# Casting the next token tile one step early in both layernorms of an adaLN transformer block

## The reference

```python
x = L0_attn_x                                            # (4, 2048, 2048) f32
mod = (_silu(L0_c) @ L0_wmod).reshape(4, 6, 1, -1)       # wmod is (2048, 12288)
sa, ca, ga, sb, cb, gb = (mod[:, i] for i in range(6))
ga = (2 * (ga >= 0) - 1) * jnp.maximum(jnp.abs(ga), 0.25)   # gb likewise
h = _layernorm(x, axis=-1) * (1 + ca) + sa
x = x + ga * _L0_attn_ref(h, W_Q, W_K, W_V, W_O)
h = _layernorm(x, axis=-1) * (1 + cb) + sb
x = x + gb * _L0_ffn_ref(h, ...)                          # 8 experts, top 2, plus shared
```

## Time and profile before

| | us |
|---|---|
| runs of before | 4077.52 and 4167.37, median 4122.44 |
| the profiled execution | 4081.17 |
| its span on the slowest core, core 7 | 4079.6 |
| spans of all cores | 4064.4 to 4079.6 |
| TensorE busy | 3369.6 (83% of the span) |
| VectorE, ScalarE, GpSimd busy | 1119.1, 641.3, 468.9 |

### The profile page before, as it was taken

One profiled execution on the slowest core, in us unless ns is written; L12 is line 12 of the kernel. 1 busy time (PEld: TensorE's weight loads), 2 busy tenths in 40 slices (PEclk: granted clock), 3 DMA queues, 4 the chain that ended last, 5 costly groups with the idle time before them and its releaser, 6 DMA issues. The chain is left out here.

```text
span 4079.6 us, 46287 instructions; the slowest of 8 cores (4064.4 to 4079.6 us)
## 1 busy us (share of the span) xinstructions
PE 3369.6 (83%) x14394; PEld 1369.0 (34%) x14394; DVE 1119.1 (27%) x2039; ACT 641.3 (16%) x1312; POOL 468.9 (11%) x891
## 2 busy tenths in 40 slices
PE   3544688888888888888894399999999999999997
PEld 0232222222222222222242144444444444444443
DVE  0255322222222222222225412122121221212212
ACT  0233222222222222222203200000000000000000
POOL 1111000000000000000010012122121221212211
PEclk8666777777777777777796599999999999999998
DMA  9999310101010101010130054555455454544544
GB/s 210 155 174 170 67 16 16 16 16 16 16 16 16 16 16 16 16 16 16 16 63 16 3 80 73 75 76 77 73 74 75 74 76 73 73 78 72 76 73 119
DMA packets 128926, 246.51 MB, mean 60 GB/s; under 512 B 15681, under 2 KB 56770, under 8 KB 126402
## 3 DMA queue, kind: packets, MB, share of 16 engines
q0 software_dynamic: 125824, 209.92, 34.1%
q1 hardware_dynamic: 2882, 33.63, 2.4%
HBM read 444.94 MB, written 8.39 MB: 111 GB/s over the span
## 5 line engine op out<-in xcount | busy, mean ns | idle before, releaser
L570 PE MATMUL pacc<-h_full,rA 128*128 128x512 bf16 x2560 | 599.7, 395 | 18.0 <-DMA rA<-wk 18.0
L1268 PE MATMUL pdn<-ysb,rD 128*128 128x512 bf16 x2560 | 571.0, 387 | 13.1 <-DVE ysb L1212 11.3
L1158 PE MATMUL px<-h,rA 128*128 128x512 bf16 x2560 | 568.3, 380 | 0.8 <-ACT comb L347 0.8
L1183 PE MATMUL px<-h,rA 128*128 128x512 bf16 x2560 | 565.6, 379 | 0.0
L570 PEld LDWEIGHTS pacc<-h_full,rA 128*128 128x128 bf16 x2560 | 256.2, 101 | 347.0 <-issue 73.6
L1268 PEld LDWEIGHTS pdn<-ysb,rD 128*128 128x128 bf16 x2560 | 253.9, 99 | 328.7 <-issue 38.9
L1200 DVE TENSOR_TENSOR ysb<-x1s,px 128x1024 bf16<-128x1024 bf16 x80 | 97.7, 1221 | 961.0 <-PE px L1183 961.0
L1158 PEld LDWEIGHTS px<-h,rA 128*128 128x128 bf16 x2560 | 251.0, 98 | 305.2 <-issue 4.9
L1183 PEld LDWEIGHTS px<-h,rA 128*128 128x128 bf16 x2560 | 250.5, 98 | 302.1
L1278 DVE SCALAR_TENSOR_TENSOR x_own<-pdn,gbcl,x_own 128x512 f32<-128x512 f32 x320 | 240.1, 750 | 345.1 <-PE pdn L1268 345.1
L1172 ACT ACTIVATE x1s<-px 128x1024 bf16<-128x1024 f32 x80 | 81.9, 1024 | 1482.1 <-PE px L1158 1482.0
(11 more groups left out here) (153 smaller groups left out, 2363.6 us busy)
## 6 DMA issues: line engine op xcount, KB each, us to landing
rB<-wmodA POOLq DMA_DIRECT2D x96, 512.0 KB, 10.2
rA<-wg POOLq DMA_DIRECT2D x128, 256.0 KB, 4.8
rA<-wu POOLq DMA_DIRECT2D x128, 256.0 KB, 4.8
rD<-wd POOLq DMA_DIRECT2D x256, 128.0 KB, 5.2
xl<-ximg SPq DMA_DIRECT2D x16, 1024.0 KB, 5.3
rA<-wk POOLq DMA_DIRECT2D x32, 256.0 KB, 4.7
rA<-wq POOLq DMA_DIRECT2D x32, 256.0 KB, 4.7
rA<-wv POOLq DMA_DIRECT2D x32, 256.0 KB, 4.7
```

Of the source, the lines that this page charges most:

```text
L570: t.matmul(pacc[:, bank * 512:bank * 512 + 512], ub[:, (dc % 8) * 128:(dc % 8) * 128 + 128], moving_fn(dc, qtr), start=(dc == 0), stop=(dc ...
L1158: lambda t, ub=ub, dc=dc, half=half: t.matmul(px1[:, half * 512:half * 512 + 512], ub[:, (dc % 8) * 128:(dc % 8) * 128 + 128], h2[:, dc * ...
L1183: lambda t, ub=ub, dc=dc, half=half: t.matmul(px3[:, half * 512:half * 512 + 512], ub[:, (dc % 8) * 128:(dc % 8) * 128 + 128], h2[:, dc * ...
L1268: t.matmul(pdn[rot][:, :], ub[:, dloc * 128:dloc * 128 + 128], ysb[:, hc * 1024 + th * 512: hc * 1024 + th * 512 + 512], start=(hc == 0), ...
```

## The change

The cast and the square are taken out of `emit_ln_piece` and become a function of their own, `emit_ln_cast`. It is called once ahead of the loop, for tile 0, and then inside piece s for tile s+1, through `precast_fn`, between the copy into `rowbf` and the broadcast. Stage a of the mod half (`fill_fn`) moves from behind the square of the mean to the place behind the new cast. The load of tile s+1 is emitted ahead of piece s, with the same wait as before: on the end of VectorE's work of piece s-1. The second layernorm gets the same early cast, without a load. The cast waits for its load and for the matmuls that read `xbf` last.

```diff
+    def emit_ln_cast(x_src_ap, xbfb, xsqb, state, extra_waits=()):
+        w_cast = list(extra_waits)
         if state.get("stats_prev"):
             w_cast.append(state["stats_prev"])
-        s_c1 = em.op("scalar", lambda s: s.activation(xbfb[:, :], x_src_ap, AF.Copy),
-                     waits=w_cast, inc=True)
+        em.op("scalar", lambda s: s.activation(xbfb[:, :], x_src_ap, AF.Copy),
+              waits=w_cast, inc=True)
         s_c2 = em.op("scalar", lambda s: s.activation(xsqb[:, :], x_src_ap, AF.Square),
                      inc=True)
-        w_mm = [s_c2, misc["CG"]]
+        state["cast_mark"] = s_c2
...
         state["rows_read"] = s_m2
-        if fill_fn is not None:
-            fill_fn()
...
         s_cv = em.op("scalar", lambda s: s.copy(rowbf[:, :], rowa[0:1, 0:512]),
                      waits=w_bc, inc=True)
+        if precast_fn is not None:
+            precast_fn()
+        if fill_fn is not None:
+            fill_fn()
         g_bc = emit_bcast(rowbf[:, :], rows_b[:, :], pbc, waits=[s_cv], bf=True)
...
+    if SUB1 >= 2:
+        xw0 = ld_x(0)
+        emit_ln_cast(xl[0][:, :], xbf[:, :], xsq[:, :], ln1_state,
+                     extra_waits=[xw0])
+    for s_idx in (range(TC) if SUB1 >= 2 else range(0)):
+        slot = s_idx % 2
+        pc = None
+        if s_idx + 1 < TC:
+            xw = ld_x(s_idx + 1)
+            nslot = (s_idx + 1) % 2
+            pc = (lambda xw=xw, nslot=nslot:
+                  emit_ln_cast(xl[nslot][:, :], xbf[:, :], xsq[:, :],
+                               ln1_state, extra_waits=[xw]))
...
+    emit_ln_cast(x_own[:, 0:2048], xbf2[:, :], xsq2[:, :], ln2_state)
     for lc in range(LC):
         src = x_own[:, lc * 2048:(lc + 1) * 2048]
+        pc2 = None
+        if lc + 1 < LC:
+            pc2 = (lambda lc=lc: emit_ln_cast(
+                x_own[:, (lc + 1) * 2048:(lc + 2) * 2048],
+                xbf2[:, :], xsq2[:, :], ln2_state))
```

More of the change, by code:

```diff
@@ L348, in emit_bcast, with emit_ln_piece @@
         return s_b
-    def emit_ln_piece(x_src_ap, dst_fn, cvec, svec_col, prow_s, prow_q, state, rows_b, pbc, t1b, xbfb, xsqb, fill_fn=None, fill_fn2=None):
-        LD = state.get("x_ready")
-        w_cast = [LD] if LD else []
+    def emit_ln_cast(x_src_ap, xbfb, xsqb, state, extra_waits=()):
+        w_cast = list(extra_waits)
         if state.get("stats_prev"):
             w_cast.append(state["stats_prev"])
-        if state.get("cast_extra"):
-            w_cast.append(state["cast_extra"])
-        s_c1 = em.op("scalar", lambda s: s.activation(xbfb[:, :], x_src_ap, AF.Copy),
-                     waits=w_cast, inc=True)
+        em.op("scalar", lambda s: s.activation(xbfb[:, :], x_src_ap, AF.Copy),
+              waits=w_cast, inc=True)
         s_c2 = em.op("scalar", lambda s: s.activation(xsqb[:, :], x_src_ap, AF.Square),
                      inc=True)
-        w_mm = [s_c2, misc["CG"]]
+        state["cast_mark"] = s_c2
+    def emit_ln_piece(x_src_ap, dst_fn, cvec, svec_col, prow_s, prow_q, state, rows_b, pbc, t1b, xbfb, xsqb, fill_fn=None, fill_fn2=None, precast_fn=None):
+        w_mm = [state["cast_mark"], misc["CG"]]
         if state.get("rows_read"):
@@ L375, in emit_ln_piece @@
         t_stats = em.mark("tensor")
+        state["stats_pp"] = state.get("stats_prev")
         state["stats_prev"] = t_stats
@@ L497, in build_nc, with ld_x @@
     x_free = [None, None]
-    for s_idx in (range(TC) if SUB1 >= 2 else range(0)):
+    def ld_x(s_idx):
         slot = s_idx % 2
@@ L503, in build_nc @@
               waits=w_ld, dma_inc=(s_x[slot], 16))
-        ln1_state["x_ready"] = (s_x[slot], x_loads[slot] * 16)
+        return (s_x[slot], x_loads[slot] * 16)
+    if SUB1 >= 2:
[11 more added lines that the diff above has]
+                               ln1_state, extra_waits=[xw]))
         def dst(dc, s_idx=s_idx):
@@ L518, in build_nc @@
                             p_rq[0:1, 0:128], ln1_state, rows_b1, p_bc1[:, :],
-                            t1sb, xbf, xsq, fill_fn=fa, fill_fn2=fb)
+                            t1sb, xbf, xsq, fill_fn=fa, fill_fn2=fb,
+                            precast_fn=pc)
         x_free[slot] = v_h
@@ L992, in build_nc @@
     v_gbcl = [em.mark("vector")]
-    ln2_state = {"mod_wait": v_cb1, "cast_extra": None}
+    ln2_state = {"mod_wait": v_cb1}
+    emit_ln_cast(x_own[:, 0:2048], xbf2[:, :], xsq2[:, :], ln2_state)
     for lc in range(LC):
         src = x_own[:, lc * 2048:(lc + 1) * 2048]
+        pc2 = None
[3 more added lines that the diff above has]
+                xbf2[:, :], xsq2[:, :], ln2_state))
         def dst2(dc, lc=lc):
@@ L1001, in build_nc @@
         emit_ln_piece(src, dst2, cb1, 48, pdn[0][0:1, 0:128], pdn[1][0:1, 0:128],
-                      ln2_state, rows_b2, pdn[2][:, :], t1f, xbf2, xsq2)
+                      ln2_state, rows_b2, pdn[2][:, :], t1f, xbf2, xsq2,
+                      precast_fn=pc2)
     h2_done = em.mark("vector")
```

## The result

The changed kernel is slower: ratio of its runs to the runs of before 1.0236, 95% interval 1.0224 to 1.0248, that is some 4176 us against 4080 (the profiled execution: 4179.27). The forecast was 4160, and 4176 is inside its range of 4110 to 4205. Of the two sides of the 2% line the prediction held the wrong one slightly likelier. The medians over all runs, 4181.97 and 4079.85, contain executions in which the clock of one die was lower, and the ratio leaves those out.

What follows compares the result with a forecast made beforehand. Mostly matmuls the change does not touch; the two layernorms are loops of waits with no engine full. 4081.2 + 60.6 (first layernorm, load in the loop) + 18.1 (second) = 4159.9, say 4160 us, range 4110 to 4205.

Steps and rivals of the forecast that it cites:

- the 2% line: Whole kernel: 4163 us, about what a measurement can tell from no change; slower by over 2% got 0.46.
- VectorE closing the loop: Second layernorm: VectorE has no idle time before the variance, so early sums gain nothing and each piece takes 2.6 us more.
- Rival D: Second layernorm does not lose because early sums shorten its loop; 4142 us or less, chance 0.05.
- period = 13.9 + L: First layernorm, pieces 1 to 14: the x load enters the loop, giving 14 periods of 22.9 us.
- L: Landing time of the x load in the first layernorm, taken as 9.0 us, bounds 5.0 and 18.5.
- Rival A: First layernorm: the load takes what it took before, 5.3 to 6.8 us; total 4108 to 4129, chance 0.22.
- Rival B: First layernorm: load there in time, VectorE closes the loop at 17.2 us; total 4080, chance 0.05.
- Rival C: First layernorm: x load served after all four modulation loads, up to 18.5 us; total up to 4293, chance 0.08.
- 144 / 41 = 3.5: First layernorm: us added to the x load if each of its 144 packets waits for one modulation packet, 41 per us.
- 334.7: First layernorm: forecast us for 14 periods of 22.9 plus a last step of 14.1, against 274.5 before.
- 0.52 for "within 2%": Whole kernel: chance given to a time within 2% of the kernel before, against 0.46 for slower by over 2%.
- The premise of one for one: First layernorm: x and modulation queues alternate packet by packet when both have work, read from 18 packets each.

Runs made afterwards that it cites:

- e2_second_only: Changed kernel with the early cast in the second layernorm only, the first layernorm as before the change; ratio 1.005 to the kernel before (4098.6 to 4102.2 us).
- e4_no_mod_loads: Changed kernel without the 64 modulation loads of the 16 pieces, whose matmuls run on what the buffers hold; 4103.36 us in one execution.
- e5_x_first: Changed kernel, but GpSimd's first modulation load of each piece also waits for the event that frees the x buffer; ratio 1.0093 (4119.4 to 4120.2 us).
- e3_free_early: Changed kernel, but the x buffer is given free after the multiply that reads it last, so its load is issued 6.7 us earlier; 4076.97 us.
- e6_rowm_later: Kernel before with only stage a of the modulation half moved behind the copy into rowbf, cast and square unmoved; ratio 0.9923 (4049.5 to 4055.6 us).
- e7_rowm_later_free: Kernel before with stage a moved behind the copy into rowbf, plus the x buffer given free after its last reading multiply; 4064.16 us, one time, inconclusive.

## Why the prediction was right, and where its sizes were off

**The second layernorm: right.** Forecast +2.6 us per piece and +18; measured 114.5 - 99.1 = 15.4 between the first and the last L432, 2.6 ahead of the first, and 0.5% in `e2_second_only`. The reason given, VectorE closing the loop, is shown by the lack of idle time ahead of the variance at 2267.67, and the added 2.6 us lie where they were put, between `rowbf` and L432 (4.80 against 2.23). Rival D falls.

**The first layernorm: the mechanism is right.** The load enters the loop in 14 pieces, and period = 13.9 + L holds. At a landing of 4.9 (`e4_no_mod_loads`) the formula gives 14 x 18.8 + 14.1 = 277.3 and the stretch took 279.6. At the 6.4 of `e5_x_first` it gives 14 x 20.3 + 14.1 = 298.3, against 299.2. In the changed kernel the 14 landings have a mean of 10.5, which gives 355.7, against 356.6. Rival A (no sharing) would have needed L under 6.8 and got 9.9. Rival B's loop of 17.2 is real, but in these runs it is there only when the load is early, as in `e3_free_early`: 14 x 17.2 + 14.1 = 254.9 us, as measured. Rival C in full (x served after all four modulation loads) falls with the 111 packets against 110, but a part of it is true, as the next paragraph shows.

**The size of L was off.** Taken: 5.0 alone, 3.5 of sharing, 0.5 for the core that ends last, 9.0 in all. Measured on the core that ended last: 13.2, 13.2, 12.3 and 10.9 for the first four of the 14 loads, then 9.3 to 10.3, with a mean of 9.8. The mis-sized term is the sum 144 / 41 = 3.5, which treated the load as sharing from its first packet on. For the load at 303.6 the runs show two parts in its place, 5.0 us together. One is standing: 3.7 us from the issue to the first packet, against 0.9 in `e4_no_mod_loads`, 2.8 more. The other is sharing: 5.9 us from the first packet to the last, against 3.7, 2.2 more, which is less than the 3.5 taken. The head start of the modulation loads was noted in the prediction ("up to 2 us ahead of it") and not priced. That the 9.0 came as near to 9.8 as it did is in part luck: 1.3 us too much for the sharing made up for about half of the missing standing.

The stretch took 356.6 - 334.7 = 22 us more than forecast. The standing and the sharing of a usual load (9.8 against 9.0) explain 14 x 0.8 = 11 us of it. The first four loads explain the other 11, and why they were slower is open. The load at 174.1 had its first packets at 178.5, 4.4 us after its issue, and then shared for some 8 us, at 16 packets per us in each queue (97 and 96 from 179 to 185), where the load at 303.6 had 28. So most of its excess is a slower transfer of both queues, not a longer standing. The 22 us would take 4160 to 4182, against the 4179.3 profiled; the stretch between the layernorms, 5 us shorter than before, is a difference that the forecast didn't have. Already L = 9.8 would have put the forecast above the 2% line (L = 9.2), so the 0.52 for "within 2%" came from this underestimate.

The premise of one for one came out right in the packet counts, but its row was thin: the 18 packets of GpSimd's queue at 10 to 15 us in the earlier trace rows held 0.00 MB together, against 1.18 MB in the 18 of the x queue, so they said nothing of how long a load waits behind packets of the size met here.

**Why the change gains so little even when the load is covered.** 254.9 against 274.5 looks like a gain of the early cast, but `e6_rowm_later` reaches 246.3 without any. Moving `rowm` away from the root is enough for the gain. The early cast puts 3.6 us of ScalarE between `rowbf` and `rows_b`, on the loop, where before those ran beside VectorE's 9 us. In the second layernorm that is a cost of 18 us, shown. In the first, 254.9 against 246.3 says 9 us of cost, but the two runs also differ in when the x buffer is freed. `e7_rowm_later_free`, which frees it as `e3_free_early` does, took 4064.16 against 4076.97 (one execution each), and those 13 us are less than the second layernorm's 18. So whether an early cast with a covered load costs anything in the first layernorm is not settled.

The Trainium skill's page "DMA: Bandwidth & Descriptors", section "Queues, rings and completion order", has each engine go round robin between queues by packets. The 111 packets against 110 agree with it; the 4 us ahead of them, in which the queue of x moved 12 packets against 183, don't follow from that rule.

## What to carry to other kernels

When an operation is moved earlier on an engine that runs its list in order, look first at what now stands behind it, and then at each of its waits: a load that had 11 us of cover had 3.4 after the move, and all of its remainder went into the loop. Price a load by what will be in the DMA queues at the instant of its new issue, not by its old landing. Try giving a buffer free at its last reader when a load stands in the loop: in the changed order one line was worth 102 us of the stretch. Where the load was covered anyway, in the order of `e6_rowm_later`, it gained nothing.

## What the runs showed of the hardware that was not expected

A load issued behind others did not start to share at once. Issued at 303.6, 1.5 us behind the first of them, it had moved 12 packets by 308, while the other queue moved 183 packets from 304 on; then both moved 111 and 110 in 4 us. It was not the kind of queue: in `e5_x_first`, where x was issued 0.5 us ahead, the modulation queue had its first packet 4.2 us after its issue. Whichever came second stood some 4 us, against some 1 us for a load with a free path. Why a load stands that long when the engines otherwise alternate between the queues, no run tells. x landed in 6.4 us when issued just ahead of the others, 9.9 behind the first two of them, and 4.9 alone.

The first landings of the changed kernel's slowest core were slower than the rest: 13.2, 13.2, 12.3, 10.9, then 9.3 to 10.3. Three other cores had 12.9 to 13.0 for the first. No run here tells why.
